# The transpositions around the attention's division, made by VectorE in 32x32 blocks instead of by TensorE

## The chip, the cores and the metric

The kernel runs on one core of a Trainium2 chip. What counts is device time of one execution, in microseconds (us). The engines of the core are TensorE (PE in the profile; its weight loads are PEld), VectorE (DVE), ScalarE (ACT), GpSimd (POOL) and SyncE (SP, which issues most DMAs). Each runs its own instructions in order and waits on semaphores for the others.

## What is computed

A gated cross-attention block and a gated quantised feed-forward block, on `x` of 8 items x 256 rows x 256 features, with 16 heads of 16 features:

```
q = layernorm(x) Wq^T,  k = ctx Wk^T,  v = ctx Wv^T         # per item 256 x 256, in 16 heads
p = softmax(where(mask, q k^T / sqrt(16), -inf))            # per head 256 x 256
x = x + tanh(g_xattn) * (concat_heads(p v) Wo^T + bo)
xn = layernorm(x);  quantise xn, w_gate, w_up, w_down to whole numbers (-128 to 127) times a scale
h = silu(xn w_gate^T) * (xn w_up^T);  quantise h by its largest magnitude
x = x + tanh(g_ffn) * (h w_down^T)
```

The masks are all true in the inputs, and the kernel takes a branch without them. The division of the softmax is done after the product with V: V carries a block of ones beside each head's 16 features, so each head's product has 32 rows, 16 of values and 16 that all hold the sum of the exponentials.

## The kernel before, in words

The kernel is written by hand for each engine. Three stages follow each other.

**Projections.** For each of the 8 items TensorE transposes the normalised rows and the context and multiplies by Wq, Wk and Wv; Q and K are split in three bf16 parts each (`parts`), written to DRAM and read back stacked over the partitions (`q_st`, `k_st`). Before, TensorE transposes the weight matrices (`weight_tr`, L1139) and ScalarE copies them out (`weight_copy`, L571); Wo is the fourth (n = 3), between items 3 and 4. GpSimd computes the inverse deviations of the layer norms (`rstd`, L430) and the lowest parts (`lo_parts`).

**Attention.** A step handles item b, in 16 heads; in the same step the row maxima of item b + 1 are computed. In each head h of step b
- TensorE computes the scores of item b for the exponential (`scores_for_exp`, L1281, bank_a, 2 banks) and the scores of item b + 1 for the maximum (`scores_for_max`, L1269, bank_b, 4 banks; head h needs the maximum of head h - 4 to be done),
- VectorE takes the maximum over each row of the latter (`maxima`, L804),
- ScalarE takes the exponential of the former (`exp`, L656).

The maxima enter the scores for the exponential through the matmul itself, as two more rows of `q_st`. For eight heads at a time, TensorE transposes them (`max_tr`, L1161), ScalarE copies them (`max_copy`, L615), GpSimd splits them in two bf16 parts (`max_split`, L474), and SyncE writes them into `q_st` by two DMAs (`max_rows`, L365). `scores_for_exp` waits for that at heads 0 and 8 (semaphores `max_in`). SyncE's queue also loads the next items' stacks (`stack_load`, L355).

Between the heads stand the other pieces of work, placed by three tables written out by hand, `PE_AT`, `DVE_AT` and `ACT_AT` (L94 to L101): head h stands for "behind the scores of head h" on TensorE and "in front of the maximum of head h" on VectorE; H + h (H = 16) means head h of the next step. For each group g of four heads: the product with V (`("pv", g)`, L1296, into bank_o, which is a single bank); ScalarE's copy of it (`("ot", g)`, L663); TensorE's transposition back to rows (`("back", g)`, L1309, into bank_m); on VectorE the reciprocal of the sums (`("rec", g)`, L894) and the product with it (`("div", g)`, L899). For all heads together: TensorE's transposition of the result (`att_tr`, L1317), ScalarE's copy of it (`att`, L669), the output projection (`out`, L1329), VectorE's residual (L906). bank_m is a single bank too: transposed maxima, transpositions back and the projection pass through it one after the other, each waiting till the last one has been read (`used`). Then VectorE takes the statistics of the new rows (`stats`, `means`), GpSimd their inverse deviation and the normalised rows (`second_rstd`, `hat`), VectorE their maxima (`row_maxima`, L934, for the item two steps back).

Step 7 has no next item: VectorE and TensorE do the feed-forward weights' rounding and transposition in its second half (`whole_weights`, `ffn_weights`). What is left of item 7 follows in the order of the tables (`leftover`).

**Feed-forward.** A maximum over all rows sets the scale; then four chunks of 512 rows through gate and up, a second scale, and the down projection.

## Time and profile before

| what | value |
|---|---|
| median of 3 runs | 284.72 us (281.92 to 285.21) |
| the profiled execution | 283.28 us, span 281.5 us |
| TensorE: matmuls, weight loads | 231.6 us (82%), 156.1 us (55%) |
| VectorE | 214.7 us (76%) |
| ScalarE | 174.4 us (62%) |
| GpSimd | 126.1 us (45%) |
| mean granted TensorE clock | 0.949 of full speed |

The span is the time from the first to the last instruction; the execution's own time has 1.8 us around it. Shares are averages over three stages with different limits. A record's duration is longer than its place in the order where instructions overlap: the distance between two starts is then the cost.

### The profile page before, as it was taken

To read this page: it belongs to the slowest core of one execution; us is meant where nothing else is said; L and a number is where in the kernel's file an instruction comes from. 1 tells how busy PE (TensorE), PEld (TensorE's weight loads), DVE (VectorE), ACT (ScalarE), POOL (GpSimd) and SP (SyncE) were. 2 spreads that over 40 slices of the span, in tenths; PEclk is the share of its full clock that TensorE was granted. 3 is DMA by queue.
4 is the path that set the end of the run, shared out by engine and by line. 5 is a ranking of instruction groups with operands and counts; after the bars stand their busy time and mean duration, and the time that the engine had idled before them with its cause. 6 is when DMAs were issued, how large, how long until landed. Compare 5 with 4: busy or idle time off the path is not lost.

```text
span 281.5 us, 6092 instructions
## 1 busy us (share of the span) xinstructions
PE 231.6 (82%) x1752; PEld 156.1 (55%) x1756; DVE 214.7 (76%) x463; ACT 174.4 (62%) x326; POOL 126.1 (45%) x203
## 2 busy tenths in 40 slices
PE   1699979989979999999998999999872488863980
PEld 1587858868646756656575666755540233322650
DVE  3469976979968697797969779799317479997992
ACT  1326466466667667775777767676941488865950
POOL 3375555543441435445373534539505153330363
PEclk9999979999999999999999999999987599997896
DMA  7829779988355445545243555000000700000199
GB/s 234 250 52 311 231 241 263 240 225 222 115 159 112 108 79 115 113 113 107 65 104 65 113 113 114 2 1 4 3 2 2 261 0 1 0 0 2 21 131 148
DMA packets 31638, 31.28 MB, mean 111 GB/s; under 512 B 5248, under 2 KB 28288, under 8 KB 31616
## 3 DMA queue, kind: packets, MB, share of 16 engines
q1 hardware_dynamic: 26832, 27.87, 38.2%
q0 software_dynamic: 1904, 1.84, 5.1%
q10 hardware_dynamic: 2880, 1.31, 1.8%
q8 instruction: 10, 0.16, 0.3%
q14 instruction: 12, 0.10, 0.1%
HBM read 20.65 MB, written 10.22 MB: 110 GB/s over the span
## 4 chain that ended last, share of the span: by engine, by line
PE 40%; DVE 18%; issue 12%; DMA 10%; ACT 6%; POOL 6%; SPq 3%; DVEq 1%; POOLq 1%; ACTq 0%
PE bank_o L1305 7%; PE bank_a L1288 6%; PE bank_b L1275 5%; PE bank_m L1331 5%; DMA x_rows<-in_x 4%; PE bank_a L1194 4%; PE bank_b L1431 3%; DMA big<-max_parts 3%; PE bank_m L1313 2%; DVE neg_max L806 2%; DVE arena L1096 2%; PE bank_o L1203 2%; DMA big<-in_ctx 2%; DVE h_max L1056 2%; ACT wgu_rows L766 1%
## 5 line engine op out<-in xcount | busy, mean ns | idle before, releaser
L806 DVE TENSOR_REDUCE neg_max<-bank_b 128x2 f32<-128x512 f32 x128 | 83.8, 680 | 14.8 <-PE bank_b L1275 11.3
L660 ACT ACTIVATE big<-bank_a 128x512 f32<-128x512 f32 x128 | 69.8, 588 | 16.0 <-PE bank_a L1288 15.3
L1288 PE MATMUL bank_a<-big 98*128 98x256 bf16 x256 | 49.0, 274 | 3.5 <-DMA big<-max_parts 2.6
L1275 PE MATMUL bank_b<-big 96*128 96x256 bf16 x224 | 42.8, 272 | 0.0
L1305 PE MATMUL bank_o<-big,v_cur 128*32 128x256 f32 x512 | 34.3, 385 | 0.8 <-ACT big L660 0.8
L1194 PE MATMUL bank_a<-arena,w_t 128*128 128x256 f32 x128 | 33.1, 408 | 0.6 <-DVE resid L817 0.5
L477 POOL CAST max_parts<-max_f 8x256 bf16<-8x256 f32 x16 | 6.4, 403 | 52.3 <-issue 49.8
L1288 PEld LDWEIGHTS bank_a<-big 98*128 98x128 bf16 x256 | 21.1, 97 | 13.6 <-ACT big L660 3.0
L1194 PEld LDWEIGHTS bank_a<-arena,w_t 128*128 128x128 f32 x128 | 25.3, 207 | 4.7 <-DVE resid L817 1.0
L450 POOL TENSOR_TENSOR arena<-resid,arena 128x512 bf16<-128x512 f32 x16 | 18.3, 1159 | 12.1 <-ACT arena L600 12.1
L1275 PEld LDWEIGHTS bank_b<-big 96*128 96x128 bf16 x224 | 21.5, 97 | 3.2 <-issue 0.2
L1305 PEld LDWEIGHTS bank_o<-big,v_cur 128*32 128x32 f32 x512 | 13.4, 109 | 13.1 <-issue 5.3
L745 ACT ACTIVATE arena<-bank_b,w_scale_x 128x512 f32<-128x512 f32 (+1 forms) x24 | 16.1, 684 | 7.0 <-PE bank_b L1431 4.5
L1431 PE MATMUL bank_b<-arena,wgu_t 128*128 (+3 forms) x61 | 17.5, 401 | 2.9 <-ACT arena L735 1.9
L552 POOL TENSOR_TENSOR big<-arena 128x512 f32<-128x512 f32 x8 | 11.1, 1389 | 19.2 <-ACT arena L749 19.2
L1450 PE MATMUL bank_b<-wd_t,arena 128*128 128x256 bf16 x96 | 15.3, 310 | 4.6 <-DVE arena L1102 4.4
L593 ACT ACTIVATE arena<-bank_a 128x512 bf16<-128x512 f32 x16 | 9.4, 596 | 15.1 <-PE bank_a L1194 10.3
L493 POOL TENSOR_SCALAR v_all<-x_rows,mv_now,rs 128x256 f32<-128x256 f32 x14 | 18.3, 1309 | 0.2 <-POOL rs L440 0.2
L1331 PE MATMUL bank_m<-w_t,arena 128*128 128x256 f32 x64 | 17.1, 413 | 1.1 <-ACT arena L671 1.1
L667 ACT ACTIVATE arena<-bank_o 128x256 f32<-128x256 f32 x32 | 12.4, 387 | 8.5 <-PE bank_o L1305 8.5
L766 ACT ACTIVATE wgu_rows<-big,magic,scal 128x768 f32 x16 | 14.8, 1014 | 4.3 <-DVE scal L1088 4.3
L560 POOL DMA_DIRECT2D out<-v_all x7 | 9.8, 1465 | 14.1 <-DVE v_all L1118 14.1
(158 smaller groups left out, 434.8 us busy)
## 6 DMA issues: line engine op xcount, KB each, us to landing
qk_parts<-arena SPq DMA_DIRECT2D x8, 768.0 KB, 4.8
big<-qk_parts SPq DMA_DIRECT2D x32, 192.0 KB, 3.7
big<-qk_parts SPq DMA_DIRECT2D x32, 128.0 KB, 3.9
x_rows<-in_x SPq DMA_DIRECT2D x8, 256.0 KB, 5.2
big<-qk_parts SPq DMA_DIRECT2D x32, 64.0 KB, 3.9
out<-x_rows SPq DMA_DIRECT2D x8, 256.0 KB, 3.1
big<-in_ctx SPq DMA_DIRECT2D x7, 256.0 KB, 5.2
out<-v_all POOLq DMA_DIRECT2D x7, 256.0 KB, 4.4
```

What stands on the lines that cost most here:

```text
L450: pool.tensor_tensor(parts[:, p, w, LO[w]], resid[:, p, w], parts[:, p, w, MID[w]], ALU.subtract).then_inc(lo_done, 1)
L493: done = pool.tensor_scalar(v_all[:, t].squeeze(1), x_rows[:, t].squeeze(1), mv2_now[:, c, 0:1], rs2[:, t], ALU.subtract, ALU.mult)
L660: act.activation(p_buf[:, h % HH], bank_a[:, h % 2].rearrange("p (c s) -> p c s", c=QC), ACT.Exp, scale=SCALE).then_inc(exp_done, 1)
L745: act.activation(silu[0:r, c % 3], bank_b[0:r, c % 3], ACT.Silu, scale=w_scale_x[0:r, c:c + 1]).then_inc(silu_done, 1)
L766: act.activation(h_round[:, q], h_all[:, :, bass.ds(t * P, P)], ACT.Identity, scale=INV_H, bias=magic[:]).then_inc(y_rounded, 1)
L806: dve.tensor_reduce(neg_max[:, p, :, h], bank.rearrange("p (c s) -> p c s", c=QC), axis=AX.X, op=ALU.max, negate=True).then_inc(max_done, 1)
L1194: last = mm(bank_a[:, w, f * S:(f + 1) * S], w_t[:, w, k, f * P:(f + 1) * P], src[:, p, k * S:(k + 1) * S], start=(k == 0), stop=(k == EC ...
L1275: done = mm(to, q_st[0:KR, p, h, c * P:(c + 1) * P], k_st[0:KR, p, h], start=True, stop=not masked)
L1288: done = mm(to, k_st[0:KM, p, h, k * P:(k + 1) * P], q_st[0:KM, p, h], start=True, stop=not masked)
L1305: done = mm(bank_o[n * 2 * D:(n + 1) * 2 * D, 0:S], v_cur[:, p, k, h], p_buf[:, h % HH, k], start=(k == 0), stop=(k == QC - 1))
L1331: done = mm(bank_m[:, c * E:(c + 1) * E], att_t[:, f, c * P:(c + 1) * P], w_t[:, 3, f], start=(f == 0), stop=(f == EC - 1))
L1431: last = mm(to, wgu_t[:, g, k, c * P:c * P + r], xq_t[:, k, bass.ds(n * CW, CW)], start=(k == 0), stop=(k == EC - 1))
```

## The change

For each group of heads VectorE now transposes the product with V in blocks of 32x32, straight out of bank_o (`turn`). A group's product has 4 x 32 partitions (head, value or sum) and 256 columns (query rows), so the four heads' blocks stand below each other, and after the block transposition partition 32n + r, block j holds query row 32j + r of head n, with its 16 values and its sums. VectorE takes the reciprocals and multiplies (`reciprocals`, `scale_heads`), two groups into one tile `att` of 256 columns, and transposes that back in blocks (`back`), right into `att_t`, which the output projection reads. The features then stand in another order, (pair of groups, head in group, group in pair, feature); GpSimd puts the rows of Wo that it takes as features into that order before they are transposed. TensorE's transpositions `back` and `att_tr` and ScalarE's copies `ot` and `att` are gone.

The tables move with it: the projection from head 7 of the next step to head 10, the residual from 8 to 12, the statistics from 10 and 11 to 13 and 14, the means from 12 to 15. `second_rstd(b - 1)` at the end of GpSimd's step b becomes `second_rstd(b - 2)` between the first split of maxima and the residual's addition of the bias. Wo's transposition and copy go from in front of item 4's projections to in front of item 6's.

```diff
-    PE_AT = {("pv", 3): H + 1, "max_tr": 1, ("back", 3): H + 3, ("pv", 0): 5, "att_tr": H + 5, "out": H + 7,
-             ("pv", 1): 9, "next_max_tr": 9, ("back", 0): 11, ("pv", 2): 13, ("back", 1): 13, ("back", 2): H}
-
-    DVE_AT = {("rec", 0): 12, ("div", 0): 13, ("rec", 1): 14, ("div", 1): 14, ("rec", 2): H, ("div", 2): H + 1,
-              ("div", 3): H + 5, ("rec", 3): H + 4, "residual": H + 8, ("stats", 0): H + 10, ("stats", 1): H + 11,
-              "means": H + 12}
-
-    ACT_AT = {("ot", 3): H + 1, "max": 1, ("ot", 0): 7, "att": H + 5, ("ot", 1): 11, "next_max": 9, ("ot", 2): 13}
+    PE_AT = {("pv", 3): H + 1, "max_tr": 1, ("pv", 0): 5, ("pv", 1): 9, "next_max_tr": 9, "out": H + 10, ("pv", 2): 13}
+
+    DVE_AT = {("turn", 0): 6, ("rec", 0): 7, ("scale", 0): 8, ("turn", 1): 10, ("rec", 1): 11, ("scale", 1): 12,
+              ("back", 0): 13, ("turn", 2): 14, ("rec", 2): 15, ("scale", 2): H, ("turn", 3): H + 2,
+              ("rec", 3): H + 3, ("scale", 3): H + 4, ("back", 1): H + 5, "residual": H + 12, ("stats", 0): H + 13,
+              ("stats", 1): H + 14, "means": H + 15}
+
+    ACT_AT = {"max": 1, "next_max": 9}
...
-        rec = sb("rec", [P, 2, QC, 4])
+        rec = sb("rec", [P, 2, NB])
...
-        o_t = part(2 * S, True).rearrange("p (a s) -> p a s", a=2)
-        att = part(2 * QC * E).rearrange("p (a c e) -> p a c e", a=2, c=QC)
+        turned = part(2 * S, True).rearrange("p (g j r) -> p g j r", g=2, j=NB)
+        att = part(S).rearrange("p (j g d) -> p j g d", j=NB, g=2)
...
+            pool.wait_ge(w_in[3], 16)
+            pool.wait_ge(w_tr, 1)
+            for f in range(EC):
+                for k in range(EC):
+                    cols = slice(k * P, (k + 1) * P)
+                    done = pool.tensor_copy(w_rows[:, 0, f, cols].rearrange("p (n g d) -> p n g d", n=4, g=2),
+                                            w_rows[:, 3, f, cols].rearrange("p (g n d) -> p n g d", g=2, n=4))
+            done.then_inc(wo_ordered, 1)
...
                 max_split(b, 1)
+                if b >= 2:
+                    second_rstd(b - 2)
...
-                if not first:
-                    second_rstd(b - 1)
...
-            weight_copy(3)
             project(4, 0, 2)
             act.wait_ge(ffn_w_in, 80)
             project(5, 1, 2, pieces=(0, 1, 2))
+            weight_copy(3)
...
+            def turn(b, g):
+
+                dve.wait_ge(pv_done, GROUPS * b + g + 1)
+                dve.transpose(turned[:, g % 2].rearrange("p j r -> p (j r)"), bank_o[:, 0:S]).then_inc(turn_done, 1)
 
             def reciprocals(b, g):
-
-                dve.wait_ge(ot_tr, GROUPS * b + g + 1)
-                chain.then(dve.reciprocal(rec[:, g % 2], rows[:, :, :, D]))
-
-            def divide(b, p, g):
+                dve.wait_ge(turn_done, GROUPS * b + g + 1)
+                chain.then(dve.reciprocal(rec[:, g % 2], turned[:, g % 2, :, D]))
+
+            def scale_heads(g):
                 chain.wait()
-                dve.tensor_tensor(att[:, p, :, 4 * D * g:4 * D * (g + 1)].rearrange("p c (h d) -> p c h d", h=4),
-                                  rows[:, :, :, 0:D],
-                                  rec[:, g % 2].unsqueeze(3).to_broadcast([P, QC, 4, D]), ALU.mult
-                                  ).then_inc(nrm_done, 1)
+                chain.then(dve.tensor_tensor(att[:, :, g % 2], turned[:, g % 2, :, 0:D],
+                                             rec[:, g % 2].unsqueeze(2).to_broadcast([P, NB, D]), ALU.mult))
+
+            def back(b, pair):
+                chain.wait()
+                if pair == 0 and not (isinstance(b, int) and b == 0):
+                    dve.wait_ge(wo_done, b)
+                dve.transpose(att_t[:, pair], att[:].rearrange("p j g d -> p (j g d)")).then_inc(at_done, 1)
...
             def weight_tr(n):
-                pe.wait_ge(w_in[n], 16)
+                if n < 3:
+                    pe.wait_ge(w_in[n], 16)
+                else:
+                    pe.wait_ge(wo_ordered, 1)
+                rows = w_rows[:, n % 3]
...
-            weight_tr(3)
             project(4, 0, 2)
...
                     if not start:
-                        pe.wait_ge(ot_done, GROUPS * b + g)
+                        pe.wait_ge(turn_done, GROUPS * b + g)
...
-                def back_tr(b, g, used):
...
-                def att_tr(b, p, used):
...
                 def project_out(b, used):
                     pe.wait_ge(*used)
-                    pe.wait_ge(at_done, b + 1)
+                    pe.wait_ge(at_done, 2 * b + 2)
...
             pe.wait_ge(full_ready, 1)
+            weight_tr(3)
             full = pe.value_load(full_rows[0:1, 0:1], min_val=0, max_val=P * S)
```

## Rows read from the trace of the kernel before

**Rows 1.** Busy times by stretch, one step: stretch, length, PE, PEld, DVE, ACT, POOL busy (instructions), PEclk, DMA share, GB/s.

```profile
161.89:178.09 16.20, 15.54 (x153) 10.39 (x154) 13.49 (x32) 11.69 (x25) 8.03 (x15) 1.00 0.46 99
```

**Rows 2.** Timeline of VectorE, maxima of heads 14 and 15 of two items: start, us, what, idle before.

```profile
89.30 1.28 DVE L806 TENSOR_REDUCE neg_max<-bank_b 128x2 f32<-128x512 f32 x2
...
187.13 1.28 DVE L806 TENSOR_REDUCE neg_max<-bank_b 128x2 f32<-128x512 f32 x2
```

**Rows 3.** Timeline of TensorE in one step (same columns).

```profile
161.79 1.96 PE L1331 MATMUL bank_m<-w_t,arena 128*128 128x256 f32 x8
163.59 0.38 PE L1288 MATMUL bank_a<-big 98*128 98x256 bf16 x2
...
164.56 1.07 PE L1305 MATMUL bank_o<-big,v_cur 128*32 128x256 f32 x16
165.56 0.38 PE L1165 MATMUL bank_m<-ident_f,neg_max 128*8 128x128 f32 x2
165.78 0.39 PE L1288 MATMUL bank_a<-big 98*128 98x256 bf16 x2
...
169.42 0.44 PE L1313 MATMUL bank_m<-ident_f,arena 128*128 128x128 f32 x2 [0.44 <-DVE arena L901]
...
170.85 0.38 PE L1288 MATMUL bank_a<-big 98*128 98x256 bf16 x2
...
173.21 0.38 PE L1165 MATMUL bank_m<-ident_f,neg_max 128*8 128x128 f32 x2
...
176.55 0.66 PE L1321 MATMUL bank_m<-ident_f,arena 128*128 128x128 f32 x4
177.05 0.39 PE L1288 MATMUL bank_a<-big 98*128 98x256 bf16 x2
```

**Rows 4.** Timeline of VectorE in the same step (same columns).

```profile
164.01 0.88 DVE L911 SCALAR_TENSOR_TENSOR x_rows<-bank_m,gate_x,x_rows 128x256 f32 x2 [1.24 <-PE bank_m L1331]
...
167.03 0.42 DVE L919 BATCH_NORM_STATS2 stats<-x_rows 128x6 f32 x1
...
170.94 1.28 DVE L806 TENSOR_REDUCE neg_max<-bank_b 128x2 f32<-128x512 f32 x2
...
172.80 0.28 DVE L901 TENSOR_TENSOR arena<-bank_m,rec 128x128 f32<-128x128 f32 x1
173.00 0.68 DVE L806 TENSOR_REDUCE neg_max<-bank_b 128x2 f32<-128x512 f32 x1
```

**Rows 5.** Timeline of all engines: one transposition of maxima to the head that needs it.

```profile
100.53 0.38 PE L1165 MATMUL bank_m<-ident_f,neg_max 128*8 128x128 f32 x2
...
102.64 1.32 SPq L369 DMA_DIRECT2D big<-max_parts  x2
...
106.04 0.39 PE L1288 MATMUL bank_a<-big 98*128 98x256 bf16 x2 [0.35 <-DMA big<-max_parts]
```

**Rows 6.** Timeline of TensorE, head 8 of step 0.

```profile
83.04 0.39 PE L1288 MATMUL bank_a<-big 98*128 98x256 bf16 x2 [1.83 <-DMA big<-max_parts]
```

**Rows 7.** Timeline of all engines, step 7 and what is left of item 7.

```profile
195.31 0.38 PE L1288 MATMUL bank_a<-big 98*128 98x256 bf16 x2
...
202.20 2.44 POOL L493 TENSOR_SCALAR v_all<-x_rows,mv_now,rs 128x256 f32<-128x256 f32 x2 [0.19 <-POOL rs L440]
...
203.89 1.07 PE L1305 MATMUL bank_o<-big,v_cur 128*32 128x256 f32 x16 [0.85 <-ACT big L660]
...
208.02 3.29 PE L1331 MATMUL bank_m<-w_t,arena 128*128 128x256 f32 x8 [0.78 <-ACT arena L671]
...
211.43 0.88 DVE L911 SCALAR_TENSOR_TENSOR x_rows<-bank_m,gate_x,x_rows 128x256 f32<-128x256 f32 x2 [4.30 <-PE bank_m L1331]
```

**Rows 8.** Timeline of GpSimd and TensorE in the projections of items 4 to 6.

```profile
51.49 0.23 POOL L433 TENSOR_SCALAR newton<-mv 128x2 f32<-128x2 f32 x1 [4.06 <-DVE mv L790]
...
53.77 2.27 POOL L450 TENSOR_TENSOR arena<-resid,arena 128x512 bf16<-128x512 f32 x2
...
61.50 0.38 PE L1183 MATMUL bank_b<-big 96*128 96x256 bf16 x2 [0.57 <-ACT arena L585]
```

67 lines of the change are left out of this document (18 added, 49 removed).

## The prediction, made before the changed kernel was run

> **What bounds the kernel now.** I read the busy times by stretch first, then TensorE's and VectorE's instructions of one step in order of time, then the chain of waits. In the attention stage a step (one batch item's exponentials, the next one's maxima) lasts 16.2 us; TensorE is busy for 15.5 of them, VectorE for 13.5, ScalarE for 11.7, and TensorE's granted clock is full [rows 1]. VectorE finishes the sixteenth row maximum of one item at 90.58 us and that of the item six steps on at 188.41 us: 16.3 us per step [rows 2].
>
> In TensorE's order [rows 3] see what a step is made of. A head costs 0.45 us (its scores for the maximum and those for the exponential; two heads stand between 163.59 and 164.56), a product with V 1.0, a transposition of the row maxima 0.22, one of a head group's result as much, that of all heads 0.5, the output projection 1.8. 16 x 0.45 + 4 x 1.1 + 2 x 0.22 + 4 x 0.22 + 0.5 + 1.8 = 15.2 us; the other 1.0 us is waits, such as 0.44 us in front of a transposition, for a division. TensorE is the bound, with little margin: VectorE is not idle because it has little to do, but because it waits for projection and scores, 1.24 us in front of the residual alone [rows 4].
>
> A second clock runs in each step. A transposed row maximum goes through ScalarE, GpSimd and a DMA before TensorE may start the eight heads that need it. In one instance the transposition starts at 100.53 us, SyncE's queue issues from 102.64, and the head starts at 106.04, released by the transfer [rows 5]: 5.5 us. In another it starts at 165.56 us and the head at 170.85 [rows 3]: 5.3 us. I take 5.4.
>
> **What the change does to TensorE.** Gone are four transpositions of a group (0.88 us), that of all heads (0.5) and the waits for divisions: 13.8 us of work are left. ScalarE loses five copies a step; it is no bound now, so I count nothing. **On VectorE** four block transpositions from PSUM and two in SBUF are added, of 128x256 each. No row shows one. What shows is the distance from one instruction's start to the next one's: 0.60 us for a maximum over 512 columns, 0.20 for a division over 128, 0.40 for half a residual (256 columns from PSUM; two last 0.88); statistics over 256 columns of SBUF last 0.42 [rows 4]. So the bounds are 0.20 (as if 128 columns) and 0.60 (as if 512); I take 0.35 for both kinds, nearest to the rows of 256 columns. The reciprocal (0.13) and the product (0.20) keep their sizes, and I cost their move from PSUM to SBUF at nothing. The next instruction starts 0.08 us before the last one's record ends: a division starts at 172.80, lasts 0.28, and the maximum behind it starts at 173.00 [rows 4]; so statistics cost 0.34 to 0.38. The Trainium skill, VectorE: DVE Perf Modes, The DRAIN you can't avoid, says instead that the next operation doesn't start until the pipeline is empty; by whole durations the step before would hold 15.6 us of VectorE instead of the measured 13.5, so the measurement decides. By its section The three transpose paths (311 ns for 128 columns of bf16) 256 columns would last about 445 ns, an estimate, which is 0.37 us from start to start.
>
> VectorE's sum per step: 16 x 0.60 maxima, 6 x 0.35, 4 x 0.13, 4 x 0.20, residual 0.80, statistics 0.76, row maximum of the normalised rows 0.60, means 0.25 + 0.18 of waiting behind a reciprocal = 15.6 us. That is below 16.3. TensorE needs 13.8, so a look at sums says faster by 0.7 a step. What decides is the order.
>
> **A step after the change, walked through.** t = 0 is the end of the sixteenth maximum. TensorE stands at head 1 of the next step by then, its product with V issued, waiting to transpose the maxima; before, it came 1.0 us late for that (173.21 against 172.22) [rows 3, 4]. It transposes; heads 2 to 7 and one product with V are 6 x 0.45 + 1.1 = 3.8 us, but head 8 may start only when the row maximum has landed: t = 5.4. Before, the projection (1.8 us) stood in this gap and hid it; the change puts it behind head 10. Step 0, which has no projection, already shows it: TensorE waits 1.83 us in front of head 8 [rows 6], most of it, though, because an older transfer stood in the queue. Then heads 8 and 9 (6.3), product with V (7.4), transposition (7.6), head 10 (8.05), ScalarE's copy of that maximum (0.8 after its transposition, 8.2), projection (10.0), scores of head 11, usable at 10.5.
>
> VectorE meanwhile does, head by head: 0.80, 0.60, 0.95, 0.73, 0.80, 0.95, 0.95, 0.73 = 6.5 for heads 0 to 7, then 0.80, 0.60, 0.95 and a reciprocal: at t = 9.0 it wants head 11's scores and waits till 10.5. **This wait of 1.5 us is new.** Four PSUM banks hold the scores and can't bridge product, transposition and projection, 3.1 us with one head between. From 10.5 on: 0.60, 1.60 (head 12 with the residual), 1.33, 1.93, 1.16 = 6.6, t = 17.1. So a step takes 17.1 us instead of 16.3.
>
> **Around it.** Of six steps between the sixteenth maxima of items 0 and 6, one has no row maximum of normalised rows (+0.2), five have it (+0.8 each): +4.2. Step 0 gains nothing on TensorE (it waits for the transfer at head 8 anyway) and VectorE gets 0.4 us more behind it: +0.4. GpSimd's inverse deviations are moved in front of the residual's addition: the same six instructions take 2.3 us from 51.49 to 53.77 [rows 8], and so put the next split of maxima about 0.7 us late; it lands at t = 13.4, when TensorE reaches the head that needs it. Hidden, without reserve.
>
> The end: before, the last product with V starts at 203.89, the last projection at 208.02, the last residual at 211.43 [rows 7], 23.0 us after 188.41. After: head 8 of step 7 at 6.5 (before at 6.9, behind the same transfer, after a projection). From there to the last product it took 8.6 us (195.31 to 203.89), 0.85 of them a wait for ScalarE, which now has less to do; without the wait and two transpositions, and with the projection that now falls here, 8.6 - 0.85 - 0.44 + 1.8 = 9.1, so 15.6 to 15.9. Product 1.1, then block transposition, reciprocal, product and block transposition in a row on VectorE, 0.41 + 0.20 + 0.29 + 0.41 and 0.06 between each, 1.6 instead of the 3.0 between 205.0 and 208.0; projection 2.0 if it still finds the full clock, as the product at 203.89 did (1.07 us, as in the step; the projection at 208.02 took 3.29 against 1.96) [rows 3, 7], 20.7. But the residual stands behind the row maxima of item 6, whose means now come at head 15, behind a product with V, a block transposition and the earlier row maxima (16.3); 16.3 + 2.3 + 2.4 (GpSimd's normalisation) [rows 7] + 0.7 = 21.7. So -1.2.
>
> The start: GpSimd's four copies of the output weights move 512 columns in all and cost 0.9 to 2.3 us (four of the shortest records there, 0.23, or the 2.27 of two operations over 1024 columns) where it is idle for 4.06 us [rows 8]. If that cover were gone, normalising item 7 would wait. Four weight transpositions (0.5 us) move on TensorE to in front of item 6's projections, where the next scores wait 0.57 us for ScalarE [rows 8]; ScalarE's weight copy goes to the same place, and the copy it would hold up waits for TensorE there. Cost 0.
>
> **Sum.** +4.2 + 0.4 - 1.2 = +3.4 us. The profiled execution took 283.28 us (span 281.5), so 286.7 (span 284.9). The median of three runs is 284.72, 1.44 above it: 288.1 us. A run differs from another by 3 us, and about 2% (5.7 us) is what a measurement here can tell from no change.
>
> **The rivals.**
> - *Starvation as walked* (0.46): 288.1; its own range 285 to 290.5 with a chain of 4.9 to 5.6 us and transpositions of 0.20 to 0.45.
> - *The chain doesn't hold head 8* (0.20): TensorE is held by the banks alone, head 8 starts at 4.3, and the wait shrinks to 0.75 us. A step is 16.4: +0.1 x 5 - 0.1 + 0.4 - 1.2 = -0.4, 284.3. Against it: the 5.3 to 5.5 us of all instances read.
> - *Block transposition costs as much as 512 columns* (0.17): two of a step's six come behind the wait and cost 0.25 more each, +0.5 a step; the four in front of it (9.0 + 1.0 = 10.0) stay within it: +2.9, 291.0; with a late split on GpSimd, 0.5 a step more, 294. It decides from 0.5 us on. This is the slower end.
> - *Faster* (0.12): transpositions at 0.20 and scores that are always there in time; VectorE's bare 15.6 - 0.9 = 14.7, +0.2 of waits: six steps of 14.9 are -8.4, less 0.6 for the step without row maxima, -1.2: 274.5. For it: TensorE has 2.5 us a step to spare. Against it: the banks, above.
> - *TensorE's clock falls* (0.05). Its busy share drops from 15.5/16.2 to about 13.8/17.1. In step 0 with its 1.83 us of idle time no matmul shows the half clock (heads after it keep their 0.39 us records) [rows 3, 6]; at half clock, as the last projection shows (3.29 against 1.96 us) [rows 3, 7], a step's 13.8 us of TensorE's work would be 23 us and the kernel over 320. The Trainium skill, TensorE: Matmul & The Clock Gate, PE-mode transpose, says that transpositions do not count as busy for the gate; taking them away would then not bring it nearer to falling. No run here shows that yet.
>
> The likeliest case gives 288.1. The range 281 to 293 holds the first two whole and most of the third, and the runs' own scatter. Faster by over 2%: 0.13 (the fourth and a little of the second). Slower by over 2%: 0.31 (the third, the fifth, and the upper side of the first). Within: 0.56.
>
> **What the profile after would show.** Block transpositions of 0.38 to 0.45 us, started 0.35 apart from their followers. Steps of 17.1 us, from one sixteenth maximum to the next. VectorE idle for 1 to 1.5 us in front of the maximum of head 11, released by TensorE's scores, and hardly elsewhere. TensorE waiting in front of head 8 for the transfer of maxima and in front of its transposition for VectorE. If steps are 16 us or less with VectorE never idle, the walk is wrong; if the idle time stands elsewhere, its order is. If the start has moved, so was my cover there.

## The result, and the profile after

The changed kernel takes 286.27 us (median of four runs, 284.47 to 544.59; without the longest, 285.49) against 283.32 for the kernel before in four runs (281.54 to 285.21): a ratio of 1.0118 (95% interval 1.0064 to 1.0172). It is about 1% slower, less than the 2% that a measurement here can tell by itself, and the interval leaves out that it is faster. The forecast was 288.1 us, within 281 to 293, and most likely no difference of over 2%. Ratios are of undisturbed runs, without the one of 544.59 us, and three of the profiles below (two late transpositions, the projection behind head 12, short transpositions alone) come from runs 1.6 to 1.8% slower than the fastest of their kernel.

The page of the kernel after: first the busy times, then the granted clock in 40 slices, then a group of VectorE's new instructions (busy time in us and mean duration in ns, idle time before them).

```profile
span 283.2 us, 5871 instructions
PE 225.0 (79%) x1660; PEld 144.3 (51%) x1660; DVE 228.3 (81%) x511; ACT 161.8 (57%) x286; POOL 127.0 (45%) x207
...
PEclk9997999999999999999999999985898599995896
...
L888 DVE STREAM_TRANSPOSE arena<-bank_o 128x256 f32<-128x256 f32 x32 | 14.0, 438 | 6.6 <-PE bank_o L1310 6.6
```

TensorE is down by 6.6 us, ScalarE by 12.6, VectorE up by 13.6; VectorE is now the busiest engine, though idle for 19% of the span. `PEclk` has an 8, a 5 and an 8 in the slices from 184 to 205 us; before, these are 9s, up to 204 us.

One step after, by the same view as [rows 1]: from one item's means on VectorE to the next's (stretch, length, PE, PEld, DVE, ACT, POOL busy, PEclk, DMA share, GB/s).

```profile
104.17:120.61 16.44, 14.84 (x144) 8.80 (x140) 15.07 (x37) 9.64 (x19) 8.04 (x14) 1.00 0.48 103
```

VectorE's order in this step: start, us, what, idle before it and its releaser. It answers to [rows 4].

```profile
106.31 0.44 DVE L888 STREAM_TRANSPOSE arena<-bank_o 128x256 f32<-128x256 f32 x1
106.67 0.65 DVE L799 TENSOR_REDUCE neg_max<-bank_b 128x2 f32<-128x512 f32 x1
...
108.71 0.43 DVE L903 STREAM_TRANSPOSE arena<-arena 128x256 f32<-128x256 f32 x1
109.07 0.65 DVE L799 TENSOR_REDUCE neg_max<-bank_b 128x2 f32<-128x512 f32 x1
...
113.57 0.18 DVE L892 RECIPROCAL rec<-arena 128x8 f32<-128x8 f32 x1
114.95 0.69 DVE L799 TENSOR_REDUCE neg_max<-bank_b 128x2 f32<-128x512 f32 x1 [1.20 <-PE bank_b L1280]
115.56 0.28 DVE L896 TENSOR_TENSOR arena<-arena,rec 128x128 f32<-128x128 f32 x1
115.76 0.87 DVE L910 SCALAR_TENSOR_TENSOR x_rows<-bank_m,gate_x,x_rows 128x256 f32 x2
```

A block transposition lasts 0.43 to 0.44 us in this step, from PSUM or from SBUF, and its follower starts 0.36 us after it. VectorE's one wait of any size in a step is that in front of head 11's maximum. It comes in all six steps, 1.01, 1.20, 1.35, 1.20, 1.35 and 1.22 us.

TensorE in the same step, answering to [rows 3, 5].

```profile
105.05 0.38 PE L1172 MATMUL bank_m<-ident_f,neg_max 128*8 128x128 f32 x2 [0.76 <-DVE neg_max L799]
...
109.65 0.39 PE L1293 MATMUL bank_a<-big 98*128 98x256 bf16 x2 [0.20 <-DMA big<-max_parts]
...
112.47 1.99 PE L1319 MATMUL bank_m<-w_t,arena 128*128 128x256 f32 x8
114.31 0.38 PE L1293 MATMUL bank_a<-big 98*128 98x256 bf16 x2
114.53 0.38 PE L1280 MATMUL bank_b<-big 96*128 96x256 bf16 x2
```

TensorE now waits for VectorE in front of the transposition of the maxima (0.76 us), hardly for the transfer (0.20); the projection stands at 112.47, in front of the scores that VectorE wants at 113.7.

**Where the 1.8 us of span went** (283.24 against 281.46). The same marks read off six traces, of four kernels, in us: "last max" is the end of the last maximum of the attention stage, "to residual" the way from there to the start of the last residual, "rest" what follows.

| kernel | last max | to residual | rest | span |
|---|---|---|---|---|
| before [rows 2, 7] | 188.41 | 23.0 | 70.0 | 281.5 |
| before, second profile | 185.87 | 21.7 | 71.6 | 279.2 |
| after | 187.54 | 24.1 | 71.6 | 283.2 |
| after, second profile | 189.49 | 24.5 | 72.4 | 286.3 |
| projection in head 7's place | 184.82 | 22.0 | 72.2 | 279.0 |
| the same, weights' rounding later | 183.62 | 19.2 | 72.6 | 275.4 |

*The start* gave 2.6 us (the sixteenth maximum of item 1 ends at 87.94 instead of 90.58), and this isn't the change. In 36 to 43 us TensorE was slower in the first profile of before (the first row) than in the one of after (the second); the second profile of before (the third) looks like after.

```profile
36.00:43.00 7.00, 5.81 (x20) 4.77 (x21) 5.68 (x11) 4.84 (x8) 3.64 (x9) 0.76 0.76 237
```

```profile
36.00:43.00 7.00, 7.00 (x41) 6.24 (x40) 6.85 (x13) 4.94 (x9) 4.68 (x10) 1.00 0.54 168
```

```profile
36.00:43.00 7.00, 7.00 (x42) 6.24 (x41) 6.85 (x13) 4.52 (x8) 4.64 (x10) 1.00 0.43 131
```

In the first, TensorE had waited 2.00 us for a load of the context (37.19), and its clock fell. *The steps* took 1.8: six in 99.6 us instead of 97.83. The first took 17.06 instead of 16.00, the five others 82.5 together instead of 81.8 (16.4 to 16.6 each; before, one of 16.87 and four of 16.2 to 16.4). *The end* took 1.1, or, by the two profiles of each, 24.3 instead of 22.4. *The rest*, which the change doesn't touch, is 70.0 and 71.6 us before and 71.6 and 72.4 after. The other profiles of this document, all of changed kernels, have 71.4 to 72.8; whether this is scatter is open.

The 1.95 us between the two profiles of after (189.49 against 187.54) are mostly step 0, which took 15.73 us instead of 14.17. In both TensorE waits 1.83 us in front of head 8, and behind that wait the granted clock fell in the second profile (the first row) and not in the first (the second row).

```profile
80.00:84.00 4.00, 3.21 (x24) 1.64 (x24) 1.50 (x3) 1.19 (x2) 0.00 (x0) 0.59 0.74 166
80.00:84.00 4.00, 3.53 (x37) 2.25 (x38) 2.49 (x6) 2.28 (x5) 0.58 (x2) 1.00 0.83 168
```

Step 0 took 15.4 to 15.7 us with a mean clock of 0.89 in five of the eleven profiles of changed kernels, and neither profile of before has it.

### The profile page after: what moved, and what is told of

Read it like the earlier page. It is cut to its first block, busy times and chain, and to the rows that moved or that the text cites. A ratio compares the mean times of both kernels' runs of the same rounds, so it can differ in the third digit from the quotient of the medians.

```text
span 283.2 us, 5871 instructions
## 1 busy us (share of the span) xinstructions
PE 225.0 (79%) x1660; PEld 144.3 (51%) x1660; DVE 228.3 (81%) x511; ACT 161.8 (57%) x286; POOL 127.0 (45%) x207
## 4 chain that ended last, share of the span: by engine, by line
issue 20%; PE 20%; DVE 13%; POOL 6%; DMA 4%; ACT 3%; SPq 1%; POOLq 1%; ACTq 0%; DVEq 0%
PE bank_m L1319 5%; PE bank_o L1310 4%; DMA big<-max_parts 4%; PE bank_a L1293 3%; PE bank_b L1415 3%; DVE arena L1099 2%; PE bank_b L1280 2%; DVE h_max L1059 2%; PE bank_a L1415 1%; ACT wgu_rows L759 1%; DVE big L1068 1%; POOL max_parts L488 1%; SPq L369 1%; DVE v_all L1121 1%; POOL big L563 1%
## 5 line engine op out<-in xcount | busy, mean ns | idle before, releaser
L799 DVE TENSOR_REDUCE neg_max<-bank_b 128x2 f32<-128x512 f32 x128 | 84.1, 673 | 12.4 <-PE bank_b L1280 9.2
L1293 PE MATMUL bank_a<-big 98*128 98x256 bf16 x256 | 50.5, 281 | 6.1 <-DMA big<-max_parts 3.7
L1310 PE MATMUL bank_o<-big,v_cur 128*32 128x256 f32 x512 | 36.0, 400 | 2.0 <-ACT big L671 1.1
L1293 PEld LDWEIGHTS bank_a<-big 98*128 98x128 bf16 x256 | 20.0, 99 | 26.7 <-ACT big L671 12.3
L1201 PE MATMUL bank_a<-arena,w_t 128*128 128x256 f32 x128 | 31.4, 392 | 0.2 <-DVE resid L810 0.2
L1201 PEld LDWEIGHTS bank_a<-arena,w_t 128*128 128x128 f32 x128 | 24.0, 197 | 3.7 <-DVE resid L810 0.6
L1415 PE MATMUL bank_b<-arena,wgu_t 128*128 (+3 forms) x64 | 18.6, 410 | 2.3 <-ACT arena L728 1.5
L563 POOL TENSOR_TENSOR big<-arena 128x512 f32<-128x512 f32 x8 | 11.1, 1385 | 19.8 <-ACT arena L742 19.8
L888 DVE STREAM_TRANSPOSE arena<-bank_o 128x256 f32<-128x256 f32 x32 | 14.0, 438 | 6.6 <-PE bank_o L1310 6.6
L1434 PE MATMUL bank_b<-wd_t,arena 128*128 128x256 bf16 x96 | 15.4, 314 | 4.4 <-DVE arena L1105 4.4
L1319 PE MATMUL bank_m<-w_t,arena 128*128 128x256 f32 x64 | 16.5, 403 | 1.6 <-DVE arena L903 1.3
L630 ACT ACTIVATE max_f<-bank_m 8x256 f32<-8x256 f32 x16 | 5.9, 370 | 20.6 <-PE bank_m L1172 20.6
L789 DVE TENSOR_SCALAR arena<-x_rows,mv,rs 128x256 f32<-128x256 f32 (+1 forms) x16 | 11.7, 769 | 7.3 <-POOL rs L440 7.3
L503 POOL TENSOR_SCALAR v_all<-x_rows,mv_now,rs 128x256 f32<-128x256 f32 x14 | 17.3, 1239 | 0.2 <-POOL rs L440 0.2
```

The source lines that it names most:

```text
L503: done = pool.tensor_scalar(v_all[:, t].squeeze(1), x_rows[:, t].squeeze(1), mv2_now[:, c, 0:1], rs2[:, t], ALU.subtract, ALU.mult)
L799: dve.tensor_reduce(neg_max[:, p, :, h], bank.rearrange("p (c s) -> p c s", c=QC), axis=AX.X, op=ALU.max, negate=True).then_inc(max_done, 1)
L1201: last = mm(bank_a[:, w, f * S:(f + 1) * S], w_t[:, w, k, f * P:(f + 1) * P], src[:, p, k * S:(k + 1) * S], start=(k == 0), stop=(k == EC ...
L1293: done = mm(to, k_st[0:KM, p, h, k * P:(k + 1) * P], q_st[0:KM, p, h], start=True, stop=not masked)
L1310: done = mm(bank_o[n * 2 * D:(n + 1) * 2 * D, 0:S], v_cur[:, p, k, h], p_buf[:, h % HH, k], start=(k == 0), stop=(k == QC - 1))
L1319: done = mm(bank_m[:, c * E:(c + 1) * E], att_t[:, f, c * P:(c + 1) * P], w_t[:, 3, f], start=(f == 0), stop=(f == EC - 1))
```

## The experiments

**The kernel before, again.**

> The kernel before, unchanged, profiled once more. In its first profile TensorE waited 2.0 us for a context load at 37.19 us and its clock fell to half behind it; the changed kernel's profile has neither and stands 2.65 us earlier at the start of step 0 (last maximum of the projections ends at 77.45 us instead of 80.08). If that lead is the change's (Wo's transposition moved), it is 80 us here again; if it is the load's chance, it is anywhere between 77 and 81 us here. Steps of 16.3 us in any case.

280.98 us, span 279.2, steps of 16.0 to 16.9 us, each within 0.03 us of the same step in the first profile. The start was 2.6 us earlier than in the first profile.

**Two more block transpositions a step, in front of the wait or behind it.** Both write a spare buffer.

```
-              ("stats", 1): H + 14, "means": H + 15}
+              ("stats", 1): H + 14, "means": H + 15,
+              ("again", 0): 7, ("again", 1): 9}      # extra_late: 13 and 15
...
+                elif what[0] == "again":
+                    dve.transpose(spare_t[:, what[1]], tg_bo[:])
```

> The changed kernel with two more block transpositions of 128x256 (SBUF to SBUF, result unused) per step on VectorE, in front of the maxima of heads 7 and 9, so ahead of the place where VectorE waits 1.2 us for head 11's scores. Theory A (the projection behind head 10 starves VectorE, the wait absorbs what stands in front of it): steps stay at 16.5 us and the wait shrinks from 1.2 to 0.5 us; 286 us. Theory B (VectorE is simply full, any of its work costs 1:1): 8 x 0.72 = +5.8 us, 292 us.

> The same two additional block transpositions, but in front of the maxima of heads 13 and 15, behind the wait. Theory A and theory B both: steps of 17.2 us, +5 to +5.8 us, 292 us. If it is free too, VectorE is no bound behind the wait either, and the walk is wrong.

Early: 287.73 us, ratio to before 1.0205 (1.0151 to 1.0259), steps of 16.49 to 16.60 us behind a first one of 17.28, as without them but for 0.2 us in the first; the wait took them in:

```profile
128.92 0.39 DVE L980 STREAM_TRANSPOSE spare_t<-tg_bo 128x256 f32<-128x256 f32 x1
...
130.81 0.43 DVE L980 STREAM_TRANSPOSE spare_t<-tg_bo 128x256 f32<-128x256 f32 x1
...
133.35 0.69 DVE L801 TENSOR_REDUCE neg_max<-bank_b 128x2 f32<-128x512 f32 x1 [0.51 <-PE bank_b L1284]
```

Late: 294.54 us, ratio 1.0424 (1.0374 to 1.0474). The last step of its profile, at full clock, took 17.1 us, 0.6 to 0.7 more, with the wait at 1.22 us. From the start of head 11's maximum to the end of the step it was 7.14 us in each of the last five steps, against 6.49 with no or with early additions. The four steps before the last took 18.6 to 19.8 us. In the first of these the clock was full, and TensorE waited 1.88 us for the transfer of the maxima, which came 4.17 us after its issue. In the three others the clock was below full, 0.83, 0.83 and 0.91. A stretch around the start of the second, and the last step:

```profile
123.00:137.00 14.00, 12.39 (x85) 7.42 (x86) 10.54 (x27) 6.35 (x13) 8.05 (x14) 0.76 0.41 85
181.00:198.00 17.00, 14.46 (x136) 8.57 (x136) 15.61 (x40) 10.03 (x19) 8.03 (x14) 1.00 0.12 23
```

So the same work is free at heads 7 and 9 and costs its 0.65 us at 13 and 15: place decides, not VectorE's sum. The early kernel's median is 1.5 us above the changed kernel's all the same. In its profile 0.2 of that are in the first step; the intervals of the two ratios overlap, so the rest need not be an effect. The late kernel's is 8.3 us above, and seven steps (0 to 6) at 0.65 us are only 4.6; the clock, below, is part of the rest.

**The chain of the maxima taken away.** Heads 8 to 15 get their scores without the two rows that carry the maximum (this part of the computation is left out), so they don't wait for the transfer.

```
-                    if h % HH == 0:
-                        pe.wait_ge(max_in[h // HH], 32 * b + 32)
+                    if h == 0:
+                        pe.wait_ge(max_in[0], 32 * b + 32)
+                    if h == H - 1:
+                        pe.wait_ge(max_in[1], 32 * b + 32)
+                    rows = KM if h < HH else KR
```

> The changed kernel; the scores for the exponential of heads 8 to 15 leave out the two rows of the maxima (96 instead of 98 rows in the matmul), and TensorE waits for their transfer only at head 15. Theory C (the transfer of the maxima holds head 8, as I walked it, and so the wait at head 11): the wait falls by 0.75 us and a step to 15.8 us. Theory A alone (the projection's place makes the wait, whatever the transfer): TensorE waits only 0.2 us for the transfer in the profile, so the wait falls by 0.2 to 0.4 us and a step stays above 16.1 us.

285.0 us in one run. The last five steps took 16.30 to 16.39 us, with a wait of 1.08 to 1.15 (the first, 18.01 us, follows a step 0 of 12.4 instead of 14.2). The chain is worth 0.15 us a step. The wait in front of head 11 is there without it.

**The projection elsewhere.** Three kernels beside one with short transpositions (all with the kernel before at 282.1 us).

```
-    PE_AT = {... "out": H + 10, ...}
+    PE_AT = {... "out": H + 6, ...}
-    ("turn", 3): H + 2, ("rec", 3): H + 3, ("scale", 3): H + 4, ("back", 1): H + 5, "residual": H + 12,
-    ("stats", 0): H + 13, ("stats", 1): H + 14, "means": H + 15
+    ("turn", 3): H, ("rec", 3): H + 1, ("scale", 3): H + 2, ("back", 1): H + 3, "residual": H + 8,
+    ("stats", 0): H + 10, ("stats", 1): H + 11, "means": H + 12
```

> The output projection is put behind head 6 of the next item instead of head 10, with VectorE's third turn, its reciprocal, product and second turn back one or two heads sooner, and the residual and statistics four to three heads sooner. Theory A (in the changed kernel a step is lengthened only by where the projection stands: TensorE issues it ahead of head 11, and VectorE, having emptied its queue of maxima, waits 1.0 to 1.35 us there): in head 7's place TensorE waits for the maxima's transfer in any case, so the projection fills that gap; the wait before head 11's maximum goes, 0.3 to 0.55 us of idle time may show before head 7's or 8's, steps are 15.4 to 15.7 us instead of 16.5, and the time is 279 to 281 us, below the changed kernel and below the kernel before. Theory B (VectorE's own work, or a fixed cost of its order, sets the step): steps stay at 16.3 to 16.6 us and the time at 285 to 287 us. A projection this early could also wait for VectorE's second turn back, in front of it on TensorE's queue all later heads: then steps grow beyond 16.8 us with a wait by the turned block.

279.97 us, ratio to before 0.9887 (0.9850 to 0.9925). Five steps are 15.66 to 15.67 us, behind a first one of 17.09:

```profile
118.22:133.89 15.67, 14.47 (x142) 8.75 (x141) 15.31 (x38) 9.64 (x19) 8.05 (x14) 1.00 0.46 103
```

VectorE is busy for 0.98 of it, and no maximum waits longer than 0.19 us for scores. Head 8 waits for nothing any more: the projection stands in front of head 7, and head 8 (112.64) follows at once. The waits for the transfer that are left, 0.19 to 0.60 us, are in front of head 0 of the next item:

```profile
104.49 0.39 PE L1293 MATMUL bank_a<-big 98*128 98x256 bf16 x2 [0.60 <-DMA big<-max_parts]
...
110.35 1.89 PE L1319 MATMUL bank_m<-w_t,arena 128*128 128x256 f32 x8
...
112.64 0.39 PE L1293 MATMUL bank_a<-big 98*128 98x256 bf16 x2
```

The gap at head 8 was real, and the projection fits in it. With the projection, VectorE's third turn, the residual and the statistics moved too, and this run by itself doesn't tell them apart; but the wait that went was one for TensorE's scores.

The other way, two heads later instead of four sooner:

```
-    "out": H + 10    "residual": H + 12, ("stats", 0): H + 13, ("stats", 1): H + 14
+    "out": H + 12    "residual": H + 14, ("stats", 0): H + 15, ("stats", 1): H + 15
```

> The output projection is put behind head 12 instead of head 10, the residual and the statistics behind heads 14 and 15. Theory A (the wait before head 11's maximum is that VectorE has worked through its queue of scores by then, since the maxima of heads 8 to 10 start only when TensorE has come past its wait for the transfer): two heads later the score banks are filled further ahead, so the wait at the projection's place is smaller, 0.5 to 0.8 us, steps 15.9 to 16.1 us, and the time 282 to 284 us. Theory B (VectorE's own work sets the step): steps 16.3 to 16.6 us, time 285 to 287 us. If the statistics crowded into heads 14 and 15 hold up the next item's first product, a wait shows on ScalarE or TensorE early in the next step and the step is as long as it was.

284.46 us, ratio 1.0056 (1.0017 to 1.0096). The last four steps took 15.95 to 16.03 us. The two before them took 16.49 and 17.31; in the longer one TensorE waited 1.55 us for the transfer of the maxima. The waits are smaller and in pieces. In that step there is one of 0.27 us in front of a maximum at 115.20, and behind it

```profile
118.12 0.45 DVE L903 STREAM_TRANSPOSE arena<-arena 128x256 f32<-128x256 f32 x1 [0.76 <-PE bank_m L1319]
119.52 0.45 DVE L888 STREAM_TRANSPOSE arena<-bank_o 128x256 f32<-128x256 f32 x1 [0.34 <-PE bank_o L1310]
```

In the last four steps only the last two are left, 0.3 to 0.4 us each.

**What the block transpositions cost.** All of them with 32 columns instead of 256, once in the changed kernel and once with the projection in head 7's place (most of the output is left out by this).

```
-                dve.transpose(turned[:, g % 2].rearrange("p j r -> p (j r)"), bank_o[:, 0:S])
+                dve.transpose(turned[:, g % 2, 0], bank_o[:, 0:32])
-                dve.transpose(att_t[:, pair], att[:].rearrange("p j g d -> p (j g d)"))
+                dve.transpose(att_t[:, pair, 0:32], att[:, 0].rearrange("p g d -> p (g d)"))
```

> All block transpositions on VectorE read and write 32 columns instead of 256; most of what the output is made of is left out by this. A transposition of 32 columns should take 0.10 to 0.20 us instead of 0.44. Theory A (VectorE has slack ahead of its wait at head 11 and only what stands behind that wait sets the step): of the six transpositions of a step the one or two behind head 11 save 0.3 us each, the wait before head 11's maximum grows from 1.2 to about 2 us, steps are 15.9 to 16.1 us, and the time is 282 to 283.5 us. Theory B (VectorE's sum of work sets the step): all six save, 1.5 to 1.8 us a step, steps are 14.8 to 15.1 us and the time is 275 to 278 us.

282.66 us, ratio 0.9995 (0.9950 to 1.0040). The last four steps took 15.97 to 16.13 us, 0.5 less, with the wait grown to 1.66 to 1.73 and more small ones. Two of the six transpositions stand behind the wait, and two times 0.23 us are that 0.5.

> The projection in head 7's place, and all block transpositions of 32 columns instead of 256; most of what the output is made of is left out by this. With the projection moved VectorE is busy 0.98 of a step of 15.66 us, and waits for nothing but 0.18 us. Theory F (with the projection moved, VectorE's sum of work is what sets the step, the block transpositions with it): the six transpositions save 0.2 to 0.3 us each, 1.2 to 1.7 us a step, of which TensorE's own work, near 14.3 us, and its wait for the transfer leave 0.7 to 1.3: steps of 14.4 to 15.0 us, time 272 to 276 us. Rival G (TensorE or the chain of the maxima sets the step of 15.66 us as well): steps of 15.3 to 15.7 us with waits before maxima grown by over 1 us, and a time of 278 to 280 us.

275.20 us, ratio 0.9775 (0.9711 to 0.9839); the last four steps took 15.05 to 15.11 us, 0.6 less. The time is as the first theory had it, the steps lie between the two. VectorE's waits for scores return, 0.65 to 1.17 us, and TensorE is busy for 14.5 us of such a step: it looks like the next bound, 0.6 us below. A short transposition lasts 0.20 us and takes 0.13:

```profile
124.48 0.20 DVE L888 STREAM_TRANSPOSE arena<-bank_o 128x32 f32<-128x32 f32 x1
124.61 0.65 DVE L799 TENSOR_REDUCE neg_max<-bank_b 128x2 f32<-128x512 f32 x1
```

Six times 0.36 - 0.13 are 1.4 us of VectorE's work a step, near the fall of 1.6 us in its busy time, from 15.31 to 13.71, between the steps of the two profiles.

**The end.**

```
-                    elif h % 2:
-                        whole_weights(h // 2)
+                    elif h == 4 or h % 2 and h > 1:
+                        whole_weights(h // 2 if h % 2 else 0)
```

> Only the rounding of the first quarter of the next layer's weights is moved on VectorE, from behind head 1 to behind head 4 of step 7. Theory D (in step 7 the third turn waits 1.9 to 2.9 us behind that rounding, TensorE with it, and this idle stretch is what stands ahead of the granted clock at half speed from 190 to 198 us): the turn and the product behind it start 2 us sooner, the clock of the stretch 190 to 198 us stays at 0.9 or more, the way from the last sixteenth maximum to the last residual shortens from 24.1 to 22 to 23 us, and the time is 284 to 285.5 us; the steps before are unchanged. Rival: the clock of step 7 falls with or without that wait; then the stretch to the last residual stays at 23.8 to 24.5 us and the time within 0.5 us of the changed kernel.

285.93 us, ratio 1.0154 (1.0095 to 1.0213), the way to the last residual 23.4 us instead of 24.1. The clock in 190 to 198 us was 0.80, so it fell here too, though less. The move did not take the wait away: the product with V came in time (189.35), but then TensorE waited 3.01 us for the transfer of the maxima, and head 8 started 6.9 us behind the last maximum, as against 6.7 without the move. The rounding lay beside both instructions of GpSimd's split of the maxima. All engines of this kernel:

```profile
188.17 1.69 POOL L487 CAST max_parts<-max_f 8x256 bf16<-8x256 f32 x1 [7.63 <-issue]
189.94 1.53 POOL L488 TENSOR_TENSOR max_parts<-max_f,max_parts 8x256 bf16<-8x256 f32 x1
191.49 1.31 SPq L369 DMA_DIRECT2D big<-max_parts  x2
...
193.97 0.39 PE L1293 MATMUL bank_a<-big 98*128 98x256 bf16 x2 [3.01 <-DMA big<-max_parts]
```

VectorE's rounding (L955, 2.02 us from 188.12) is beside it. In a step of the changed kernel these two take 0.39 and 0.66 us (106.00, 106.47). In step 7 of the changed kernel the rounding is beside them as well, and they take 0.76 and 1.53 us; in the kernel before, 0.64 and 1.54. The Trainium skill, GPSIMD Engine Reference, in its table of specifications, says that GpSimd's SBUF interfaces are shared with VectorE and contend with VectorE's instructions in a two-port mode or with two SBUF inputs. By that, longer times beside a pass over SBUF are expected, though the table gives no size; this trace agrees, with 3.2 us instead of 1.05.

> The projection in head 7's place, and with it the rounding of the first weights moved in step 7 from behind head 1 to behind head 4. In the kernel with the projection alone moved, the second turn back of step 7 ended at 189.47 us because the rounding of 2.9 us stood in front of its product, and TensorE waited 1.13 us for it ahead of the projection at 189.61 us, ScalarE 2.72 us for its next scores. Theory E (that wait lies on the way to the last residual): the projection starts near 187.6 us, the way from the last sixteenth maximum to the last residual shortens from 22.0 to 20 to 21 us, steps stay at 15.0 to 15.7 us, and the time is 277.5 to 279.5 us. Rival: the rounding then holds up the products and weight transpositions behind it by as much; the way stays at 21.5 to 22.5 us and the time at 279.5 to 280.5 us.

277.79 us, ratio 0.9886 (0.9829 to 0.9942). Here the projection started at 187.11 and the way to the last residual was 19.2 us, shorter than either theory had it (20 to 21); the clock stayed full until the residual. That is one profile. The ratio is the same as without the move (0.9887), so a further gain is not shown by the times.

> The changed kernel once more, for a second profile. If the fall of the granted clock in step 7 belongs to the change, TensorE's clock is again below 0.7 of full speed somewhere in 188 to 200 us, and the way from the last sixteenth maximum to the last residual is 23.5 to 24.5 us; if it was chance, the clock is full there and the way 22 to 23 us. The steps are 16.4 to 16.6 us with 1.0 to 1.35 us idle before head 11's maximum in either case.

288.79 us, one run, span 286.3. The last five steps were 16.44 to 16.59 us, and the waits 1.01 to 1.35; the way to the residual was 24.5 us, and the clock fell again (0.71 in 190 to 198 us).

## Why the prediction was right, and where it wasn't

**Block transpositions: right.** Taken at 0.35 us from start to start and forecast to last 0.38 to 0.45; measured 0.36 and 0.43 to 0.44. The rival of 512 columns (0.5 us and more) is out. The estimate of 445 ns and 0.37 us, from the figure for bf16 in the Trainium skill, VectorE: DVE Perf Modes, The three transpose paths, agrees with the trace as well. That records overlap does not stand against the section The DRAIN you can't avoid of the same page of the Trainium skill, as I had put it: it says too that a next operation that isn't held starts earlier, and starts 0.36 us apart under records of 0.44 us fit that.

**The wait in front of head 11's maximum: right in place and releaser**, forecast 1.5 us, measured 1.0 to 1.35. The cause I gave was half right. I had two things make it, the transfer that holds head 8 and the projection behind head 10. Without the transfer's hold the wait was still 1.08 to 1.15 us; with the projection behind head 6 it was gone, and two more transpositions in front of it were free. The projection's place is the cause.

**The chain of the maxima: mis-sized.** Taken as 5.4 us, measured 4.6 (105.05 to 109.65). The way through ScalarE and GpSimd is the same, 2.1 us to SyncE's issue (100.53 to 102.64 in [rows 5], 105.05 to 107.15 after); it is the transfer that took 2.5 us from issue to head instead of 3.4. I had read the 5.4 us off the wrong rows: both instances [rows 3, 5] are transpositions behind head 9, for head 0 of the next item, and the second wasn't released by a transfer at all. The one instance before of a transfer that head 8 waited for [rows 6] was issued at 80.55 and took 2.5 us to 83.04, as the transfers for head 8 do after (2.5 to 2.6 us); the one of after with 3.4 us is again for head 0 (131.38 to 134.76). Why some take longer, up to 4.17 us in the kernel with late transpositions, is open. In the changed kernel the transposition waits for VectorE's sixteenth maximum instead. The rival in which the chain doesn't hold head 8 gave 16.4 us a step; the measured 16.4 to 16.6 is its number, reached with my wait.

**The length of a step: too long**, 17.1 us against 16.5. From the transposition to head 11's maximum it took 9.9 to 10.05 us instead of 10.5, since the chain is 0.8 shorter, and from there to the end of the step 6.5 instead of 6.6. VectorE's sum is 15.1 instead of 15.6 (15.07 of busy time in 16.44), but what is saved in front of the wait gives nothing. So the five steps with the row maxima cost +0.14 each on average (16.51 instead of 16.37), and not +0.8.

**The first step: it doesn't start as I had it.** It took 17.06 us, 1.06 more than before; I had 16.5. The walk begins with TensorE ready at the end of the sixteenth maximum. Here that maximum ended at 87.94, and TensorE came to the transposition 1.1 us later:

```profile
89.07 0.38 PE L1172 MATMUL bank_m<-ident_f,neg_max 128*8 128x128 f32 x2
```

From there on it is a step like the others: 10.0 us to head 11's maximum, then 5.9 (6.5 less the row maximum). In the later steps the transposition starts 0.06 us behind the maximum. That one lateness is more than half of the +1.8 us that the steps cost, and TensorE brings it from step 0, where it waits 1.83 us in front of head 8.

**The product with the reciprocals: a cost at nothing that wasn't, but on no path.** I wrote that it costs nothing more when its input moves from PSUM to SBUF. One instance of 32 did, in the first step:

```profile
91.11 1.27 POOL L514 TENSOR_TENSOR x_rows<-x_rows,tg_bo 128x512 f32<-128x512 f32 x1
91.21 1.33 DVE L896 TENSOR_TENSOR arena<-arena,rec 128x128 f32<-128x128 f32 x1
```

Before, the longest of the 32 took 0.29 us, though in six steps one lay within the same addition, with one of its inputs in PSUM:

```profile
94.03 1.27 POOL L502 TENSOR_TENSOR x_rows<-x_rows,tg_bo 128x512 f32<-128x512 f32 x1
94.72 0.28 DVE L901 TENSOR_TENSOR arena<-bank_m,rec 128x128 f32<-128x128 f32 x1
```

With both in SBUF it ended 0.16 us after GpSimd's addition; in the other steps of this kernel the two don't meet. It did not lengthen the first step: it stands in front of the wait at head 11, which was still 1.01 us, and in the kernel with two late transpositions it took only 1.03 us and the stretch from the transposition to head 11's maximum was 10.04 us all the same. With the projection early, where VectorE is full, one of the four products of each step took 0.56 us beside GpSimd's split.

**Step 0's 0.4 us didn't come**: step 0 took 14.17 us in both first profiles. In the second profile of after it took 15.73, for another reason, the clock.

**The end: wrong sign.** Forecast -1.2 us against before, measured +1.1 (+1.9 by two profiles of each). The part that I worked out is there: block transposition, reciprocal, product, block transposition start at 207.62 and are over at 209.11, 1.5 us; and the last residual stands behind item 6's row maxima.

```profile
209.25 1.97 PE L1319 MATMUL bank_m<-w_t,arena 128*128 128x256 f32 x8 [1.26 <-DVE arena L903]
...
211.06 0.69 DVE L935 TENSOR_REDUCE row_max<-v_all 128x2 f32<-128x512 f32 x1 [1.95 <-POOL v_all L503]
211.66 0.87 DVE L910 SCALAR_TENSOR_TENSOR x_rows<-bank_m,gate_x,x_rows 128x256 f32<-128x256 f32 x2
```

What I missed lies ahead of that. In step 7 the block transposition of group 0 stands behind the rounding of the weights, and TensorE behind it:

```profile
187.66 2.02 DVE L955 TENSOR_SCALAR wgu_b<-wgu_rows 128x2560 bf16<-128x2560 f32 x2
189.60 0.88 DVE L955 TENSOR_SCALAR wd_b<-wd_rows 128x1408 bf16<-128x1408 f32 x1
190.40 0.43 DVE L888 STREAM_TRANSPOSE arena<-bank_o 128x256 f32<-128x256 f32 x1
```

```profile
190.98 1.94 PE L1310 MATMUL bank_o<-big,v_cur 128*32 128x256 f32 x16 [0.89 <-DVE arena L888]
```

Before, ScalarE copied bank_o and nothing of this stood behind VectorE. Head 8 of step 7 came at 6.7 us even so, near the 6.5 of the forecast. The term that failed is the 9.1 us from there to the last product with V: it took 12.2 (194.24 to 206.48; 11.7 in the second profile). I had taken ScalarE's 0.85 us out of it, and a wait of 1.06 us for ScalarE stood there again (206.48); and I had it at full clock, while a product and the projection in it took 0.86 and 0.6 us longer. I walked VectorE's queue through a step with maxima, and for step 7 only from the last product with V on. The clock, by stretch:

```profile
186.00:190.00 4.00, 1.88 (x14) 0.75 (x10) 3.83 (x9) 1.89 (x4) 1.28 (x2) 0.93 0.00 0
190.00:198.00 8.00, 6.76 (x50) 3.12 (x50) 4.64 (x14) 3.29 (x7) 7.29 (x10) 0.50 0.01 3
```

In the stretch in front of the fall TensorE was busy for 1.9 of 4 us, and then it had half the clock, 1.2 of 2.4 GHz, for 8 us: the product with V took 1.94 us for 1.07. Before, it was busy for 5.4 of the 6 us from 184 to 190 and the clock held. With the projection early and the rounding later it was busy for 5.0 of these 6 us, and the clock held too; that kernel's way to the residual is 5 us shorter. This is no rule yet: with the projection early alone, TensorE was busy for 3.5 of the 6 us, and the clock held from 190 to 198 us all the same, and fell only in front of the last projection (3.65 us instead of 1.97). Of the profiles whose steps were not much longer, all seven with the projection behind head 10 or 12 have a clock of 0.50 to 0.80 in 190 to 198 us, and all five with it behind head 6 or 7 have 1.00. That the rounding's wait makes the clock fall is not shown: with the rounding later and the projection behind head 10 it still fell, to 0.80.

**The clock as a rival.** I gave 0.05 to a fall in the steps and over 320 us. In the changed kernel steps 1 to 6 don't show it, but step 0 does in the second profile (0.59 in 80 to 84 us) and cost 1.6 us; I had argued from the first profile of before that TensorE's 1.83 us of idle time there leave the clock full. In the kernel with two late transpositions the clock fell in three steps (0.83, 0.83 and 0.91 on average), which are 1.5 to 2.7 us longer than the last, at full clock. The kernel's four other runs, which have no profile, had mean granted clocks of 0.906 to 0.915, also below the changed kernel's 0.931 to 0.949. I had set against a fall that, by the Trainium skill, TensorE: Matmul & The Clock Gate, PE-mode transpose, transpositions don't count as busy, so that taking them away brings a fall no nearer. The section says this of a transpose mode of the matmul, and no view of the profile tells whether this kernel's transpositions run in it. The traces speak against relying on it: the changed kernels have fewer transpositions, and the clock fell in their step 0 or step 7 where that of before was full. What else changed with them (waits and their places) isn't told apart by these runs.

**The start** was forecast to stay, and it did: GpSimd's four copies of the output weights took 1.25 us in a stretch where it then idled for 0.86.

```profile
46.72 1.25 POOL L475 COPY arena<-arena 128x128 f32<-128x128 f32 x4
48.83 0.23 POOL L433 TENSOR_SCALAR newton<-mv 128x2 f32<-128x2 f32 x1 [0.86 <-DVE mv L783]
```

That the median fell near the forecast is in large part luck: the sum of +3.4 us was made of +4.6 for the steps and -1.2 for the end, and the measured one of +1.8 and +1.1 to +1.9, 2.9 to 3.7 in all. The start (-2.6) and the rest (+1.5), which the forecast left out, make up the remainder of the profiles' +1.8. The two errors cancelled; the medians can't show that, only the traces do.

## What to carry to other kernels

The change removed 6.6 us of work from the engine that bounded the steps, and the kernel became about 1% slower, in large part because the same change put the projection where VectorE starves and left the gap at head 8 empty; the same transpositions with the projection in the gap make it 1.1% faster than before. When work moves from one engine to another, set the order anew: ask at each wait what could stand in it, and test a place by adding the same instruction ahead of the wait and behind it, since here one was free and the other cost its full length. And look at the odd steps, first and last, for what stands in front of the moved work on its new queue, and for an engine that comes late into them.

## What the runs showed of the hardware

- A 32x32 block transposition of 128x256 fp32 takes 0.36 us of VectorE's time, 128x32 takes 0.13: about 1.0 ns per column beyond 32 (0.23 us for 224), from PSUM as from SBUF.
- A short operation on VectorE with both inputs in SBUF took 1.33 us instead of 0.28 beside a GpSimd addition of 1.27 us; with one input in PSUM, in the kernel before, it took 0.28 within the same addition, in six steps. In the eleven profiles of changed kernels the same instance took 1.03 to 1.96 us. GpSimd's second instruction on 8x256 took 1.5 to 1.9 us instead of 0.66 beside VectorE's rounding, before as after, and both together 3.2 instead of 1.05 where both lay beside it. Here the move of an operand from PSUM to SBUF moved it into this contention.
- TensorE's clock fell in step 7 behind a stretch in which the engine was busy for 1.9 of 4 us, and stood at half for 8 us (0.71 in the second profile): two products with V and a projection there took 0.87, 0.86 and 0.6 us more each than at full clock.
- One and the same program shows a fall of the clock in one execution and not in the other: step 0 of the changed kernel, behind the same wait of 1.83 us, took 14.17 us at 1.00 and 15.73 at 0.89.
- Two DMAs of 4 KB each took from 2.5 to 4.2 us from issue to the start of the matmul that waited for them.
